# Splitting the routing work over loop steps and reordering the experts of a decoder layer on one core

## The reference, cut to what matters

```
x = x + layernorm(attention(layernorm(x)))           # 16 heads, causal, rope
t = layernorm(x)                                     # 2048 tokens x 256
logits = t @ router                                  # 8 experts, the best 2 of each token
C = 640                                              # slots of an expert, filled in order of tokens
buf[e, pos] = t[token]                               # tokens over 640 are dropped
h = silu(buf @ gate[e]) * (buf @ up[e])              # 176 wide
out_buf = h @ down[e]
y = sum_k weight_k * out_buf[e_k, pos_k] + shared_mlp(t)     # shared part 704 wide
x = x + layernorm(y)
```

## Time and profile before

| | |
|---|---|
| median of 3 runs | 814.61 us (809.74 to 817.81) |
| the profiled execution | 814.12 us, of which its span from first to last instruction 812.3 us |
| PE busy | 758.1 us (93%) |
| DVE busy | 600.9 us (74%) |
| POOL busy | 562.1 us (69%) |
| ACT busy | 502.4 us (62%) |
| mean granted clock of PE | 0.975 |

### The profile page before, as it was taken

The page is one execution under the profiler, slowest core; times in us unless marked ns, Lnnn a source line. Parts: engine busy times, 40 slices in busy tenths (PEclk is TensorE's granted clock), DMA queues, the critical chain, the costliest instruction groups (busy, mean ns, idle before and its releaser), DMA issues.

```text
span 812.3 us, 14115 instructions
## 1 busy us (share of the span) xinstructions
PE 758.1 (93%) x4364; PEld 631.7 (78%) x4364; DVE 600.9 (74%) x1590; ACT 502.4 (62%) x1171; POOL 562.1 (69%) x465
## 2 busy tenths in 40 slices
PE   5899999999999999999899999899899999999876
PEld 4677778888888888887688888788687888887543
DVE  6648877767897877889988988998663277773266
ACT  5687777776777777666668776576432465542242
POOL 4767898878889887877889987798440544416721
PEclk9999999999999999999999999999999999999885
DMA  9311245422222221221122212221250434523421
GB/s 312 110 41 52 68 159 176 158 75 69 66 66 68 64 71 62 69 63 53 60 84 75 90 64 69 59 68 64 66 153 7 165 126 168 188 78 105 123 65 52
DMA packets 47733, 75.74 MB, mean 93 GB/s; under 512 B 9712, under 2 KB 24624, under 8 KB 47664
## 3 DMA queue, kind: packets, MB, share of 16 engines
q1 hardware_dynamic: 43504, 65.19, 24.9%
q0 software_dynamic: 3072, 8.39, 3.2%
q10 hardware_dynamic: 1088, 1.31, 0.5%
HBM read 57.71 MB, written 17.17 MB: 92 GB/s over the span
## 4 chain that ended last, share of the span: by engine, by line
PE 70%; DVE 8%; POOL 7%; ACT 6%; issue 6%; DMA 1%; DVEq 0%; ACTq 0%; POOLq 0%
PE ps L430 19%; PE ps L976 14%; PE ps L941 12%; PE ps L992 9%; PE ps L962 7%; PE ps L1138 6%; POOL o_lo L1778 2%; POOL q_sw L1764 1%; POOL q_sw L1756 1%; POOL kh_row L1773 1%; ACT prob L643 1%; POOL q_lo L1768 1%; POOL slot_inputs L1794 1%; DVE hid_both L1652 1%; DVE hid_hi L1642 1%
## 5 line engine op out<-in xcount | busy, mean ns | idle before, releaser
L643 ACT ACTIVATE prob<-ps,neg_max 128x512 f32<-128x512 f32 (+3 forms) x256 | 132.6, 526 | 68.6 <-DVE neg_max L1321 68.6
L976 PE MATMUL ps<-pt,vp 128*128 128x512 f32 (+3 forms) x512 | 149.1, 434 | 8.0 <-issue 6.4
L976 PEld LDWEIGHTS ps<-pt,vp 128*128 128x128 f32 x512 | 82.5, 190 | 56.8 <-issue 25.4
L1321 DVE CUSTOM_DVE_ANT_0 ps<-ps,causal_row 128x512 f32<-128x512 f32 (+3 forms) x256 | 117.3, 520 | 0.0
L1778 POOL TENSOR_TENSOR o_lo<-o_t,o_hi 128x512 fp32r<-128x512 f32 x64 | 87.3, 1364 | 34.0 <-ACT o_hi L671 32.9
L1768 POOL TENSOR_TENSOR q_lo<-q_sw,q_hi 128x512 fp32r<-128x512 f32 x62 | 83.8, 1352 | 37.4 <-ACT q_hi L665 37.1
L962 PE MATMUL ps<-id_f,prob 128*128 128x128 f32 x640 | 92.3, 275 | 2.3 <-ACT pt L652 2.3
L941 PE MATMUL ps<-k_hi,q_hi 128*128 128x512 f32 x248 | 87.1, 351 | 2.5 <-issue 2.0
L1334 DVE TENSOR_SCALAR pt<-ps,vcol 128x384 f32<-128x384 f32 (+2 forms) x192 | 81.8, 476 | 9.7 <-PE ps L962 9.7
L1764 POOL TENSOR_TENSOR q_sw<-q_cos,q_sw 128x512 f32<-128x512 f32 x62 | 79.0, 1275 | 14.1 <-DVE q_cos L1313 6.0
L1756 POOL TENSOR_TENSOR q_sw<-q_sw,rope_sb 128x512 f32<-128x512 f32 x64 | 82.6, 1291 | 4.1 <-ACT q_sw L632 3.8
(11 more groups left out here) (219 smaller groups left out, 1970.9 us busy)
## 6 DMA issues: line engine op xcount, KB each, us to landing
kh_row<-kvh_rows SPq DMA_DIRECT2D x64, 256.0 KB, 3.1
inv_row<-inverse_sums SPq DMA_DIRECT2D x64, 256.0 KB
slot_inputs<-zeros SPq DMA_DIRECT2D x8, 640.0 KB, 4.9
xg<-slot_inputs SPq DMA_DIRECT2D x8, 640.0 KB, 4.8
slot_outputs<-yo SPq DMA_DIRECT2D x8, 640.0 KB, 3.3
up_raw<-in_w_up_dram SPq DMA_DIRECT2D x8, 368.0 KB, 4.8
wo_raw<-in_wout_dram SPq DMA_DIRECT2D x4, 512.0 KB, 7.8
dn_sb<-in_w_dn_dram SPq DMA_DIRECT2D x8, 256.0 KB, 3.6
```

Of the source, the lines that this page charges most:

```text
L643: ins = act.activation(prob[:, i % 2, ROW_AT[nt]:ROW_AT[nt] + w], ps_s[bank][:, at:at + w], ACT.Exp, scale=-1.0, bias=neg_max[:, i % 2, nt ...
L976: ins = pe.matmul(ps_qo[:, mt * P:SEQ], vp[:, b * TPB + mt, :], pt[:, i % 2, cols], start=(mt == 0), stop=(mt == PT_BANKS[-1][-1]))
L1321: ins = dve.tensor_tensor_reduce(s_, s_, causal_row[:, (NT - 1 - nt) * P:], 1.0, BIG, ALU.add, ALU.min, neg_max[:, i % 2, nt:nt + 1])
```

## The change

- DVE's routing of batches 0 and 1 is cut from three parts into seven, at n = 7 (maxima), 8 (their numbers), 9 (marks), 10 (counts), 13 (positions), 14 (slots to fill) and 15 (slots to read; for batch 1 in 14 as well). `positions` on PE moves from n=9 to 11. The scatters of batch 0 start at n=15 instead of 11; those of batch 1 are all started after the loop, where before six of the eight were inside it.
- At the start PE turns batch 0 tile by tile as each is ready, and `gates` of batches 0 and 1 use a new order, `low_parts_last`: the four products that need only the high parts of the tokens first, then, after a wait, the two with the rests.
- The experts: `expert_down(e)` comes after `expert_up(e+1)` and `turn_slots(e+2)`. `hid_hi`, `hid_lo` and `hid2_both` become two sets. The first group of each expert uses `low_parts_last`. DVE makes both gated products of a half before it splits them, and the rests of the next inputs before the last split. ACT, SP and POOL follow: `down_head(e)` stands ahead of the Silus of e+1, and `rest_of_down(e)` behind `split_up(e+2)`. The last two `expert_down` stand one behind the other.

```diff
-        hid_hi, hid2_both, hid_lo = (place(n, at + k * CAP * 4, [CAP], F32R) for k, n in enumerate(("hid_hi", "hid2_both", "hid_lo")))
+        hid_hi, hid2_both, hid_lo = ([place(f"{n}{r}", a + k * CAP * 4, [CAP], F32R) for r, a in enumerate(hid_at)]
+                                     for k, n in enumerate(("hid_hi", "hid2_both", "hid_lo")))
...
-        TURN_LOGITS, POSITIONS = 6, 9
+        TURN_LOGITS, POSITIONS, SLOTS = 6, 11, 13
+        SCATTER_AT = [15, 16, 17, 18, 19, 20, 22, 23]
...
-            at = [route_step(b) + n for n in SCATTER_AT]
+            at = [UNITS if b else route_step(b) + n for n in SCATTER_AT]
             return [m for m in range(2 * TPB) if at[m] == i or (i == UNITS and at[m] >= UNITS)]
...
+        def low_parts_last(pe, psum, w_hi, w_lo, m_hi, m_lo, low, n):
+            for o in range(EO):
+                pe.matmul(psum, w_hi(o), m_hi(o), start=(o == 0), stop=False)
+                pe.matmul(psum, w_lo(o), m_hi(o), start=False, stop=False)
+            pe.wait_ge(low, n)
+            for o in range(EO):
+                last = pe.matmul(psum, w_hi(o), m_lo(o), start=False, stop=(o == EO - 1))
             return last
...
+            def load_next(e, r):
+            def store_outputs(e):
+                sp.wait_ge(yo_ready, 3 * e + 6)
+                sp.dma_start(yg_dram[bass.ds(e * CAP, CAP), :].rearrange("(p s) e -> p s e", p=P), yo) \
+                    .then_inc(yo_stored, 16)
+            load_next(0, 0)
+            with sp.Fori(0, NE // 2 - 2) as pair:
+                for k in range(2):
+                    load_next(pair * 2 + (k + 1), 1 - k)
+                    store_outputs(pair * 2 + k)
+                    load_down(pair * 2 + (k + 2), k)
...
-                    act.wait_ge(rows_known, 1)
+                    act.wait_ge(rows_known, 1) if tiles[0] >= 2 else act.wait_ge(token_psum, 1)
...
             expert_head(0)
+            silus_of(0)
+            expert_head(1)
             with act.Fori(0, NE // 2 - 1) as pair:
-                expert_steps(pair * 2, False)
-            expert_steps(NE - 2, True)
+                for k in range(2):
+                    down_head(pair * 2 + k, k)
+                    silus_of(pair * 2 + (k + 1))
+                    expert_head(pair * 2 + (k + 2))
+                    outputs_of(pair * 2 + k)
+            down_head(NE - 2, 0)
+            silus_of(NE - 1)
+            outputs_of(NE - 2)
+            down_head(NE - 1, 1)
+            outputs_of(NE - 1)
...
+                if b == 0:
+                    for t in range(TPB):
+                        pe.wait_ge(xn_ready, t + 1)
+                        for o in range(EO):
+                            ins = pe.transpose(ps[TURN_BANKS[b][o]][:, t * P:(t + 1) * P],
+                                               xn[:, b % 2, t, o * P:(o + 1) * P], id_f[:])
+                            if t == TPB - 1:
+                                ins.then_inc(xt_psum, 1)
+                    return
...
+                cols = slice(2 * P, 3 * P)
+                if b < 2:
+                    pe.wait_ge(xt_hi_ready, (b + 1) * EO)
+                    low_parts_last(pe, ps[GATE_BANK[b]][:], lambda o: w0_hi[:, o, cols], lambda o: w0_lo[:, o, cols],
+                                   lambda o: xt_hi[:, o, tok(b)], lambda o: xt_lo[:, o, tok(b)], xt_lo_ready, (b + 1) * EO) \
+                        .then_inc(gate_psum, 1)
+                    return
...
+                    if c == 0 and k == 0:
+                        low_parts_last(pe, ps[3][:, 0:HC], lambda o: w_hi_[:, o, a:z], lambda o: w_lo_[:, o, a:z],
+                                       lambda o: xg_hi[:, o, cs], lambda o: xg_lo[:, o, cs], xg_ready, 3 * e + 2) \
+                            .then_inc(gu_psum, 1)
+                        continue
...
+            def expert_ups(e, r):
+                pe.wait_ge(xg_hi_ready, 3 * e + 2)
+                pe.wait_ge(up_ready, e + 1)
+                expert_up(e, r, 0)
+                pe.wait_ge(xg_ready, 3 * e + 3)
+                expert_up(e, r, 1)
...
+            expert_ups(0, 0)
+            turn_slots(1, 1)
             with pe.Fori(0, NE // 2 - 1) as pair:
-                expert_steps(pair * 2, False)
-            expert_steps(NE - 2, True)
+                for k in range(2):
+                    expert_ups(pair * 2 + (k + 1), 1 - k)
+                    turn_slots(pair * 2 + (k + 2), k)
+                    expert_down(pair * 2 + k, k)
+            expert_ups(NE - 1, 1)
+            expert_down(NE - 2, 0)
+            expert_down(NE - 1, 1)
...
+            def their_numbers(g):
...
+            def as_columns(g):
...
+            def count_chosen(g):
...
+            def choose(g):
+                best_experts(g)
+                their_numbers(g)
+                as_columns(g)
+                count_chosen(g)
+            def take_positions(g):
...
+            def slots_to_fill(g):
...
+            def slots_to_read(g):
...
                     elif n == TURN_LOGITS + 2:
-                        choose(b)
-                    elif n == POSITIONS + 1:
-                        find_slots(b)
+                        their_numbers(b)
+                    elif n == TURN_LOGITS + 3:
+                        as_columns(b)
+                    elif n == TURN_LOGITS + 4:
+                        count_chosen(b)
+                    elif n == SLOTS:
+                        take_positions(b)
+                    elif n == SLOTS + 1:
+                        slots_to_fill(b)
+                        if b:
+                            slots_to_read(b)
+                    elif n == SLOTS + 2 and b == 0:
+                        slots_to_read(b)
...
-            best_experts(ROUTED)
             choose(ROUTED)
             dve.wait_ge(scattered[1], 2 * TPB * 16)
             shared_hidden(0, [0, 1])
...
+            def gated(e, c):
+                m = 2 * e + c
+                dve.wait_ge(silu_ready, 2 * m + 1)
+                dve.wait_ge(gu_psum, 3 * m + 2)
+                dve.tensor_tensor(hid[:, c, :], sg[:, c, :], ps[4][:, 0:HC], ALU.mult).then_inc(gu_free, 1)
+                dve.wait_ge(silu_ready, 2 * m + 2)
+                dve.tensor_tensor(hid2[0:H2, c, :], sg2[0:H2, c, :], ps[5][64:64 + H2, 0:HC],
+                                  ALU.mult).then_inc(gu_free, 1)
+            def split_gated(e, r, c):
+                m = 2 * e + c
+                cs = slice(c * HC, (c + 1) * HC)
+                dve.wait_ge(gu_free, 2 * m + 4)
+                dve.tensor_copy(hid_hi[r][:, cs], hid[:, c, :]).then_inc(hid_hi_ready, 1)
+                dve.tensor_copy(hid2_both[r][0:H2, cs], hid2[0:H2, c, :]).then_inc(hid_hi_ready, 1)
+                dve.wait_ge(hid_hi_ready, 2 * m + 1)
+                dve.tensor_tensor(hid_lo[r][:, cs], hid[:, c, :], hid_hi[r][:, cs].bitcast(F32),
+                                  ALU.subtract).then_inc(hid_ready, 1)
+                dve.wait_ge(hid_hi_ready, 2 * m + 2)
+                dve.tensor_tensor(hid2_both[r][LO:LO + H2, cs], hid2[0:H2, c, :],
+                                  hid2_both[r][0:H2, cs].bitcast(F32), ALU.subtract).then_inc(hid_ready, 1)
...
-            dve.memset(hid2_both[32:LO, :].bitcast(F32), 0.0).then_inc(pad_ready, 1)
-            dve.wait_ge(pad_ready, 2)
+            dve.memset(hid2_both[1][32:LO, :].bitcast(F32), 0.0).then_inc(pad_ready, 1)
+            dve.wait_ge(sy_psum, 2 * B)
+            dve.memset(hid2_both[0][32:LO, :].bitcast(F32), 0.0).then_inc(pad_ready, 1)
+            dve.wait_ge(pad_ready, 3)
             expert_rest(0)
+            gated(0, 0)
+            split_gated(0, 0, 0)
+            gated(0, 1)
+            expert_rest(1)
+            split_gated(0, 0, 1)
             with dve.Fori(0, NE // 2 - 1) as pair:
-                expert_steps(pair * 2, False)
-            expert_steps(NE - 2, True)
+                for k in range(2):
+                    gated(pair * 2 + (k + 1), 0)
+                    split_gated(pair * 2 + (k + 1), 1 - k, 0)
+                    gated(pair * 2 + (k + 1), 1)
+                    expert_rest(pair * 2 + (k + 2))
+                    split_gated(pair * 2 + (k + 1), 1 - k, 1)
+            gated(NE - 1, 0)
+            split_gated(NE - 1, 1, 0)
+            gated(NE - 1, 1)
+            split_gated(NE - 1, 1, 1)
...
-            for e in range(NE + 1):
+            for e in range(NE + 2):
                 if e < NE:
                     split_up(e, e % 2, e < 2)
-                if e:
-                    rest_of_down(e - 1, (e - 1) % 2)
+                if e > 1:
+                    rest_of_down(e - 2, e % 2)
```

More of the change, by code:

```diff
@@ L818, in expert_head, with silus_of, outputs_of @@
                     act.copy(xg_dst(xg_hi, dst), xg_src(bank)).then_inc(xg_hi_ready, 1)
[L820 to L835 removed]
+            def silus_of(e):
+                for c in range(2):
+                    act.wait_ge(gu_psum, 3 * (2 * e + c) + 1)
```

(14 more changed lines are left out.)

112 lines of the change are left out of this document (31 added, 81 removed).

## The result

The kernel became slower by 0.6%: 819.16 us (median of 20 runs, 816.36 to 822.71) beside 815.62 for the kernel before (20 runs, 809.74 to 820.62), ratio 1.0057 with a 95% interval of 1.0038 to 1.0075 (the two medians alone give 1.0043, 3.5 us). The forecast of 805.7 and its range miss it. The profiled execution has a span of 819.0 us, 6.7 more than before; about 3 of the 6.7 lie in which executions were profiled, for the change's took 1.7 more than its median and the one before 1.5 less.

The account below looks back on a forecast made before the run. TensorE (PE) was taken to bound nearly every stage. From 814.1 us: -0.9 start, -6.2 routing, -1.5 key split, +5.0 scatters after the loop, +1.7 clock, -6.5 experts gave 805.7, range 798.5 to 813.5.

Parts of the forecast that it names:

- The routing: Attention loop: seven parts remove most of the four bursts' 7.4 us loss, leaving 0.6 a batch; gain 6.2 us.
- routing still pays: Rival, chance 0.13: in the loop as_columns and slots_to_fill each stall a step as bursts did; 811.9 us.
- The key split: Loop: k_lo on DVE beside the first scatter loses 2.26 us; 0.8 of it was left, gain 1.5.
- Scatters after the loop: After the loop: eight scatters on POOL delay inverse_std2, and PE waits; cost 5.0 us, between 4 and 6.5.
- the clock: Behind PE's new idle time after the loop: 3.41 us at half speed; cost 1.7 us, 0 to 6.8.
- The experts: Expert stretch: DVE gets a whole expert's gates for its splits; gain 6.5 us, between 3 and 8.
- The filling: Start of the experts: expert 1's gates follow its own turning and wait; 0.9 us lost, 0 to 1.6.
- the second half of the gates: In each expert: it needs Silu and a DVE product early; 0.1 us each, 0.7 in seven.
- The end: Last expert_down: split output weights have one buffer, so PE waits 3.5 us with the signals.
- the rival with both gaps: Rival, chance 0.08: idle gaps after the loop and at the last expert each cost 6.8 us by slow clock; 817.6.
- The start: Kernel start: with low parts last, gates start at about 10.8 instead of 11.69; gain 0.9 us, 0 to 1.5.

Follow-up runs that it names:

- the old routing: Changed kernel with choose and find_slots again as two bursts at their old steps and all scatters in the loop; 812.34 us, ratio 0.9974.
- the bursts with the repaired experts: Changed kernel with earlier burst routing, two sets of split output weights, a last-output buffer, first gated products ahead of splits; 806.75 us, ratio 0.9897.
- the scatters in the loop: Changed kernel with batch 1's eight scatters issued in the loop's last three steps; 810.19 us, ratio 0.9936.
- DVE's order turned: Changed kernel with an expert's first gated products ahead of the previous expert's second-half splits on DVE; 816.72 us, ratio 1.0014.
- the bursts with halves: Changed kernel with earlier burst routing, repaired expert order and buffers, and POOL's q_sw and kh_row products halved around bursts; 806.56 us, ratio 0.9893.
- with two sets: Changed kernel with a second set of the output weights' split parts for the last expert; 817.09 us, ratio 1.0012.
- POOL's work cut short: Changed kernel with POOL's q_sw and kh_row cut from 512 to 32 columns in routing steps, the rest left out; 812.32 us in one run.
- `q_cos` first: Changed kernel with earlier burst routing and DVE making q_cos ahead of each burst instead of behind it; 819.7 us in one run.

## Why the prediction was wrong

**The routing, -6.2 forecast: the step that failed.** "At least 0.8 of the 2.67 was already covered; and the step ahead now does less. I leave 0.6 a batch, between 0 and 1.86, and nothing for the other parts, which are shorter than what a burst had covered." It takes a part's length as its own. The earlier trace rows already held the contrary: 1.24 us for four elements. The length belongs to POOL, so it isn't divided when the work is; it is paid again in each step that has a part. Over the plain step of 7.96, the four steps with a burst, those beside them and the key split's had lost 9.9 us; after the change ten steps lose 9.0. The "nothing for the other parts" failed too: the counts of batch 1 alone make a step of 9.53. The rival "routing still pays" (0.13) had the loop's result and half of the reason ("DVE is so full"); I should have given it the larger chance, as its own row said that these instructions wait.

The Trainium skill ("SBUF — State Buffer", Who interferes with whom) says that an instruction of VectorE with two inputs in SBUF, or in one of the two-port fast modes, contends with a GpSimd instruction that reads SBUF, and that one with a single input outside these modes doesn't. The traces agree in part: `gap`, `oh`, `chosen` and the counts take 1.05 to 1.25, the cast to `top_f` (0.17) and `max_index` (0.15) don't wait. But `keep`, with one input, takes 1.27 in the change and 0.16 before, and no trace says in which mode it ran. The prediction drew on this page, and that seven parts pay such waits more often than three bursts, and then gave it no price.

**The key split, -1.5.** Its step did go from 10.22 to 7.96. But it goes with the old routing too (7.96) and comes back with other edits (9.02, with `k_lo` at 3.77, in the run of the bursts with the repaired experts): not the work of this change. What decides how long it stalls isn't shown.

**Scatters after the loop, +5.0, and the clock, +1.7: right.** 4.41 and 0.36 of waiting, 1.9 by the clock. That the clock's 1.7 came so near is luck: the fall was 6.82 us long and not 3.41, and PE stood still through part of it. The place, the queue and the chain through `inverse_std2` were as forecast, and the run with the scatters in the loop shows it.

**The experts, -6.5: the mechanism was right, two terms were mis-sized.** The filling, put at 0.9, lost 5.3: from 651.20 to 672.09 are 20.9 us, where PE's work is 15.6. The wait that the prediction named there, behind the second expert's turning, did take 0.9. What failed is "the second half of the gates, which needs Silu and a DVE product early", put at "0.1 each (0 to 0.5, an estimate)". I had followed ACT and PE through the filling, and not DVE's list, in which the four splits come ahead of the gated product; a wait and restart of 2.1 came from that and, in the profiled execution, half speed worth 1.6. Both went in the run with DVE's order turned. The end, "PE waits 3.5 with the signals", measured 3.2 with its wait, but 1.6 more by half speed behind it. The turns between took 9.6 to 10.2 us where 9.35 had been counted, 2.0 in five. I had priced the clock at one gap alone; the rival with both gaps (0.08) was nearer in kind, though each fall cost 1.6 to 1.9 and not 6.8.

**The start, -0.9:** gates at 10.91 in place of 11.69, 0.8, and 0.6 at the loop's first step. Right, but below what runs of the whole kernel can tell: that step came between 69.90 and 73.17 in the thirteen traces whose code is the same up to there, the change's own and those of the runs with its start. Three of them have the same two stretches of 3.41 us at 0.50 ahead of the loop as the kernel before, and there it comes at 71.5 to 71.9, 0.5 to 1.0 earlier than 72.48.

## What to carry to other kernels

When a short instruction takes far longer than its elements, find on the other engine the instruction whose end it ends with. If it is always there, cutting the work into parts pays the wait in more places; cut the neighbour's instructions (not below the size at which it becomes the bound), or put all of the small ones where the neighbour stands still (not tried here). When a pipeline is deepened, walk every engine's list through the first and the last turn, the splits and copies included: here the two ends lost 5.3 and 5.0 us in the profiled execution, and the eight waits that went had been 5.5.

## What the hardware showed that I had not expected

- DVE beside POOL: a wait usually ends with POOL's running instruction, but `k_lo` waited through four of them (4.96) and with bursts and repaired experts 3.77, each time beside a scatter. It isn't the split alone: in the bursts with halves it was `var_eps`, a four-element instruction with one input, that took 3.87 there.
- A length of idle time doesn't say whether the clock falls. The 1.9 us in the experts' filling were followed by 0.50 in the change and with two sets, and not in the six other traces that have this wait. A wait of 1.6 near the loop's end, which the kernel before has too, was followed by 0.50 for 3.41 us in two runs (POOL's work cut short, `q_cos` first) and not in the others.
- The start of the kernel differs by 3.3 us between profiled executions of the same code, with a stretch at 0.50 that is 3.41 or 6.83 long and in most of them a second one (the one at 57.77 in the earlier trace rows is such). The loop's first step follows them: it comes at 69.9 to 70.1 with one stretch of 3.41, at 71.5 to 71.9 with two, and at 72.5 to 73.2 with 6.83 and 3.41. Part of the spread of the runs can come from it.
